# Holding the fourth chunk's query and key writes until the first head's maxima rows have landed, with unread matrix products in the prologue's last units

## Chip, core and metric

One core of one Trainium2 chip. The metric is the device time of one launch in microseconds (us). Times of single instructions are in us on the profile's own scale, which begins with the first instruction.

## What is computed

A transformer block on x of 2 x 1024 x 256 (B = 2, S = 1024, H = 256): modulation vectors from a small input c, a layer norm with scale and shift, causal attention with 16 heads of width 16, a gated residual, a second modulated layer norm, and a mixture of 16 experts (4 chosen for each token, plus a shared one) with a second gated residual.

```python
h = _layernorm(x) * (1 + ca) + sa
q, k, v = split(h @ W_qkv.T + b_qkv, 3)            # 16 heads of width 16
scores = where(causal, -inf, (q @ k.T) * scale)
x = x + ga * ((softmax(scores) @ v) @ W_out.T + b_out)
h = _layernorm(x) * (1 + cb) + sb
x = x + gb * moe(h)                                # routed experts + shared expert
```

## The kernel before

All 2048 tokens are on one core, cut into four chunks of 512 (NC = 4), chunks 0 and 1 for batch 0, chunks 2 and 3 for batch 1. The instructions are written by hand, one program for each engine, with semaphores between them; each engine runs its own program in order. SP (SyncE) has nothing but transfers and waits in its program: `dma_start` puts a transfer into SP's queue (q1 in the profile), and a `wait_ge` in front of it stops everything behind it in that program. ScalarE (ACT) has a queue of its own (q10), and uses it for three transfers only, below.

**Prologue** (from 0 to 89 us). For each chunk TensorE (PE) turns the normed tokens and makes the query and key projections, four tiles of 128 features x 512 tokens per chunk, each from 6 products of 512 columns (L2085, `hh` and `hl` are the high and low part of the activations, `Wqkh` and `Wqkl` of the weights). The results are split into three bf16 parts in the tile AP (`PT[c % 2]`), and SP writes each tile as three transfers of 384, 256 and 128 KB to the DRAM tensor qk_parts (`write_tile`, L795), so 12 transfers and 3 MB for a chunk. From there they are read back, head group by head group, as Qs and Ks (`stage`, L802 and L803). There are 8 head groups of four heads; groups 0 to 3 need chunks 0 and 1 alone.

**Attention** is one loop over the head groups n = 0 to 7, with two interleaved streams on PE in an order worked out beforehand: the `scores` of group n (L2166), whose exponentials ACT makes (L1377) and whose products with the values (`products`, L2152) follow, and the `score_unit`s of group n+1 (L2060 for the causal mask, L2062), 48 for each group, of which VectorE (DVE) only takes the row maxima (L1517). The maxima are turned by PE (`turn_max`, L2130), copied by DVE to the tile MT (L1633), and three small transfers of 4 KB (`aug`, L728) write them as three further rows under the queries in Qs, so that the scores come out with the maximum taken off. This is done for each half of the queries: `aug_in[slot][half]` counts the landings. A score of the first half waits for `aug_in[slot][0]`, and the first score of the second half (step s = 4 of 12) for `aug_in[slot][1]`.

For group 0 no attention runs beside the units: 36 of the 48 are interleaved with chunk 3's projections, and the last 12 (u = 36 to 47) stand alone, in the part `n == -1` of PE's body. In it the first half's maxima are turned after unit 40; ACT issues their three transfers on its own queue, while SP issues those of every other half.

SP's order around this place is: the 12 writes of chunk 2, the 12 of chunk 3, a wait until all of these have landed (L912), then Wg (L913) and three broadcast loads of the modulation rows (L916, 256 KB each), and then the first thing of attention, the maxima rows of group 0's second half (L728). After these come the loads for group 2.

A bank of PSUM, `pvb`, holds the sums of `products`; the first product of a group overwrites it. In the prologue it was used for the values, which were read by DVE before unit 41.

Of the kernel before, what the change touches and what calls it, by code (L numbers as in the profile page):

```python
# [15 lines left out]
P = 128  # L16
# [7 lines left out]
TPC = CH // P  # L24
HG = 4
# [67 lines left out]
UNITS = len(ROWS) * HG  # L93
# [60 lines left out]
OVER = PER * (4 * KH + 4)  # L154
# [19 lines left out]
}  # L174


IDLE_PE = {1: 16, 13: 10, 19: 4}


# [150 lines left out]
def program(nc, x, wqk, bqk, wv, bv, wout, bout, cT, wmod, wgate, wsh, wexp, qkd, modrows, hTd, xd, padd, zd, wd, out):  # L330
    with ExitStack() as ctx:

        def sem(name):
            return ctx.enter_context(nc.semaphore(name))
# [75 lines left out]
        hh = [early.put(f"hh{i}", [P, KH, CH], F32R) for i in range(2)]  # L410
        hl = [early.put(f"hl{i}", [P, KH, CH], F32R) for i in range(2)]
        Rq = [early.put(f"Rq{i}", [P, CH], F32) for i in range(2)]
        Wqkh, Wqkl = (early.put(n, [P, KH, 2 * H], F32R) for n in ("Wqkh", "Wqkl"))
# [108 lines left out]
        mbank, ebank, pvb, tb = allb[0:RING], allb[RING:2 * RING], allb[6], allb[7]  # L522
# [44 lines left out]
        aug_in = [[sem(f"aug_in{i}_{h}") for h in range(2)] for i in range(SLOTS)]  # L567
# [195 lines left out]
        def _(sp):  # L763
# [20 lines left out]
            def write_parts(c):  # L784
                for i in range(4):
                    write_tile(c, i)

            def write_tile(c, i):
                b, half, m = c // (S // CH), c % (S // CH), M_ORDER[i]
                sp.wait_ge(parts_done[b], 4 * half + i + 1)  # L790
                rows = qkd[m // KH, b, (m % KH) * P:(m % KH + 1) * P, :, half * CH:(half + 1) * CH]
                for first, count, part in PART_RUNS[m // KH]:
                    src = PT[c % 2][:, part:part + 1, m, :].broadcast_to([P, count, CH]) if m // KH else (
                        PT[c % 2][:, part:part + count, m, :])
                    sp.dma_start(rows[:, first:first + count, :], src).then_inc(parts_out[c % 2], 16)  # L795

            def stage(n, slot):

                q, k = (qkd[t].rearrange("b (g j d) i s -> (b g) (d i) j s", g=NG, j=HG)[n:n + 1].rearrange(
                    "a d j s -> (a d) j s") for t in range(2))  # L800
                for half in range(S // CH):
                    sp.dma_start(Qs[slot][0:NPR, half, :, :], q[:, :, half * CH:(half + 1) * CH]).then_inc(staged[slot], 16)  # L802
                sp.dma_start(Ks[slot][0:NPR, :, :], k).then_inc(staged[slot], 16)  # L803
# [85 lines left out]
            def body(n, at, first, last):  # L889
                if n == -1:  # L890

                    write_parts(0)
                    write_tile(1, 0)
                    write_tile(1, 1)
                    sp.wait_ge(parts_out[0], 16 * 12)
                    sp.wait_ge(parts_out[1], 16 * 6)
                    stage(0, 0)
                    write_tile(1, 2)
                    write_tile(1, 3)
                    stage(1, 1)  # L900
                    sp.wait_ge(v_read, 2 * (S // CH))
                    sp.wait_ge(const_done, N_CONST)
                    for s in range(SLOTS - 1):
                        stage_values(s, s)
                    sp.wait_ge(modrow_step, 7)
                    sp.dma_start(modrows, MR).then_inc(modrow_out, 16)

                    write_parts(2)
                    write_parts(3)
                    for i in range(2):  # L910
                        sp.wait_ge(parts_out[i], 16 * 12 * B)
                    sp.wait_ge(v_read, 2 * NC)  # L912
                    sp.dma_start(Wg[:, :, :], wgate).then_inc(wg_in, 16)  # L913
                    sp.wait_ge(modrow_out, 16)
                    for i, dst in enumerate((SBr, CBr, GBr)):
                        sp.dma_start(dst[:, :, :], modrows[:, i * H:(i + 1) * H].rearrange(  # L916
                            "(a b) h -> a b h", a=1).broadcast_to([P, B, H])).then_inc(modrow_in, 16)
                    return
                slot = at(0)[0]
                sp.wait_ge(bank_read["t"], USE[("max", n, 1)][1] + 1)  # L920
                aug(sp, slot, 1)
                for k in EARLY_LOADS.get(n, ()):
                    load_words(k)
                if n + SLOTS - 1 < NIT:

                    sp.wait_ge(e_ps, n * HEADS + 1)
                    sp.wait_ge(pv_done, n * NS + 1)
                    stage(n + (SLOTS - 1), (slot + SLOTS - 1) % SLOTS)
                    stage_values(n + (SLOTS - 1), (slot + SLOTS - 1) % SLOTS)
                for k in EARLY_RAW.get(n, ()):  # L930
                    load_raw(k)
                if not last:
                    sp.wait_ge(bank_read["t"], USE[("max", n + 1, 0)][1] + 1)
                    aug(sp, (slot + 1) % SLOTS, 0)
                if n == 0:
                    keep_pads()
                for k in EARLY_STORES.get(n, ()):
                    store_words(k)
                if n == 5:
                    for k in range(3):  # L940
                        load_words(k)
                if n in (5, 6):
                    store_turned(n - 5)
                if n == 7:
                    load_turned(0)
                    load_turned(1)
# [1073 lines left out]
        def _(pe):  # L2020
# [50 lines left out]
            for c in range(NC):  # L2071
# [7 lines left out]
                for i, m in enumerate(M_ORDER):  # L2079
                    n = 4 * c + i  # L2080
                    if n >= QK_RING:
                        pe.wait_ge(qk_read, 2 * (n - QK_RING + 1))
                    for k in range(KH):
                        for a, (w, h) in enumerate(((Wqkh, hh), (Wqkh, hl), (Wqkl, hh))):
                            ins = nc.tensor.matmul(allb[QK_RING + n % QK_RING], w[:, k, m * P:(m + 1) * P],  # L2085
                                                   h[c % 2][:, k, :], start=(k == 0 and a == 0),
                                                   stop=(k == KH - 1 and a == 2))
# [12 lines left out]
                for v in range(2):  # L2100
                    if c:
                        pe.wait_ge(v_read, 2 * (c - 1) + v + 1)
                    for u in range(2):
                        t0 = (2 * v + u) * P
                        for k in range(KH):
                            for a, (h, w) in enumerate(((hh, Wvh), (hl, Wvh), (hh, Wvl))):
                                ins = nc.tensor.matmul(allb[6 + v][:, u * H:(u + 1) * H], h[c % 2][:, k, t0:t0 + P],
                                                       w[:, k, :], start=(k == 0 and a == 0),
                                                       stop=(k == KH - 1 and a == 2))
# [15 lines left out]
            def turn_max_waits(n, half):  # L2125
                pe.wait_ge(mp_step, n * 9 + (9 if half else 4))
                before(pe, ("max", n, half))

            def turn_max():
                nc.tensor.transpose(tb.bitcast(BF16)[0:3 * HG * TPC, 0:P],  # L2130
                                    MP[:, :, :, :].rearrange("p a j i -> p (a j i)"), identb[:, :]).then_inc(mpT_ps, 1)
# [116 lines left out]
            def work(piece):  # L2248
# [15 lines left out]
                if what == "tab":  # L2264
                    spread_tables()

            def body(n, at, first, last):
                if n == -1:
                    for u in range(OVER, UNITS):
                        score_unit(0, 0, u)  # L2270
                        if u == max(OVER, HG * TPC) + HG:
                            pe.wait_ge(v_read, 2 * NC)
                            turn_max_waits(0, 0)
                            turn_max()
                    pe.wait_ge(qk_read, 2 * 4 * NC)
                    return
                (slot, turn), (nxt, nxt_turn) = at(0), at(1)
                pe.wait_ge(staged_v[slot], turn * 16 + 16)
                if not last:
                    pe.wait_ge(staged[nxt], nxt_turn * (16 * STAGE_DMAS) + 16 * STAGE_DMAS)  # L2280
                if last:
                    pe.wait_ge(m_red, NIT * UNITS)
                for what, i in ORDER:
                    if what == "scores":
                        scores(n, slot, turn, i)
                    if what == "unit" and not last:
                        score_unit(n + 1, nxt, i)
                    if what == "products":
                        if i == 0:
                            turn_max_waits(n, 1)  # L2290
                        if i == 5 and not last:
                            turn_max_waits(n + 1, 0)
                        if i >= 0:
                            products(n, slot, i)
                        elif n:
                            products(n - 1, at(-1)[0], NS - 1)
                    if what == "max" and (i == 1 or not last):
                        turn_max()
                    if what == "out" and (not last if i == 0 else n):
                        turn_out(2 * n - i)  # L2300
                    if what == "late":
                        if last and i == LAST_OUT:
                            turn_out(2 * n)
                        for piece in LATE_PE.get((n, i), ()):
                            work(piece)
# [66 lines left out]
            def idle_products(s):  # L2372
# [4 lines left out]
                else:  # L2377
                    was_read(pe, ("cnt",))
                    to = allb[0]
                for i in range(IDLE_PE[s]):  # L2380
                    nc.tensor.matmul(to[:, :], Wsh[:, 0:P], Wsh[:, P:P + CH], start=True, stop=True)

            for s in range(-1, SN):
                if s >= 0:
                    (s_multiply if S_ORDER[s][0] == "u" else s_down_tiles)(*S_ORDER[s][1:])
                if s in IDLE_PE:
                    idle_products(s)
# [140 lines left out]
```

## Time and profile before

| | |
|---|---|
| time of three runs | 651.31 us median (649.25 to 651.44) |
| span of the profiled execution, first to last instruction | 644.6 us |
| its own time | not given by the page; 6.7 us lie between its span and the median |
| busy in the span | PE 90%, DVE 76%, ACT 59%, POOL 52% |
| packets of SP's queue | 45.3% of the 16 DMA engines' time |
| last score unit of the prologue starts | 85.68 us |
| first score of attention starts | 89.32 us |
| first score of the second half starts | 99.47 us |

The shares are averages over the whole span. Around 60 to 87 us the DMA engines are full; at 86 to 89 us PE has nothing to run.

### The profile page before, as it was taken

How to read it: one execution, taken by the hardware profiler on the slowest of the kernel's cores; microseconds unless marked ns; L12 is line 12 of the kernel's file. 1: busy time of each engine (PE TensorE's matmuls, PEld its weight loads, DVE VectorE, ACT ScalarE, POOL GpSimd, SP SyncE). 2: the span in 40 equal slices, each digit the busy share in tenths (PEclk: the TensorE clock that was granted, in tenths of full speed). 3: DMA queues.
4: the chain of work that ended last, by engine and by line, in shares of the span. 5: the costliest groups of instructions: out<-in, count | busy, mean ns of one | idle time of the engine just before them, and what ended most of it. 6: DMA issues, size and time to landing. Idle time of an engine off the chain costs nothing. (4 is left out here: it accounts for less than half of the span.)

```text
span 644.6 us, 13664 instructions
## 1 busy us (share of the span) xinstructions
PE 582.1 (90%) x3960; PEld 395.7 (61%) x3960; DVE 487.5 (76%) x1415; ACT 382.8 (59%) x926; POOL 337.9 (52%) x585
## 2 busy tenths in 40 slices
PE   3879879999999999998997799997799999999996
PEld 3657533434343444444342378776799999999985
DVE  4888978888888868776967568898566766666648
ACT  3546437666766656655858552643356777776662
POOL 5524614455747527763738876774144444444430
PEclk9989969999999999998999989999799999999999
DMA  8349965961707273451305243665964444444498
GB/s 270 137 158 288 334 221 151 243 210 71 216 26 224 87 209 141 136 185 63 118 34 174 77 150 115 232 217 207 364 220 134 135 135 134 133 135 134 126 374 335
DMA packets 69066, 113.62 MB, mean 176 GB/s; under 512 B 12578, under 2 KB 51106, under 8 KB 67844
## 3 DMA queue, kind: packets, MB, share of 16 engines
q1 hardware_dynamic: 62036, 93.74, 45.3%
q0 software_dynamic: 6864, 19.01, 7.6%
q8 instruction: 34, 0.56, 0.4%
q14 instruction: 36, 0.29, 0.1%
q10 hardware_dynamic: 96, 0.01, 0.0%
HBM read 60.57 MB, written 49.94 MB: 171 GB/s over the span
## 5 line engine op out<-in xcount | busy, mean ns | idle before, releaser
L1377 ACT ACTIVATE Pr<-bank 128x512 f32<-128x512 f32 (+3 forms) x384 | 165.5, 494 | 94.8 <-PE bank L2166 91.1
L1517 DVE TENSOR_REDUCE mxA<-bank 128x1 f32<-128x128 f32 (+3 forms) x256 | 112.2, 484 | 23.9 <-PE bank L2062 23.7
L1233 POOL DMA_INDIRECT expert_rows<-Y,YIX x79 | 75.7, 959 | 104.0 <-DVE ytmp L1938 75.5
L2166 PE MATMUL bank<-Qs,Ks 99*128 99x512 bf16 (+3 forms) x384 | 118.6, 332 | 8.0 <-ACT Pr L1377 3.8
L2062 PE MATMUL bank<-Ks,Qs 96*128 96x512 bf16 (+3 forms) x384 | 122.1, 334 | 2.2 <-DVE mxA L1517 1.3
L1517 DVE TENSOR_REDUCE mxB<-bank 128x1 f32<-128x512 f32 x128 | 81.5, 681 | 13.5 <-PE bank L2062 13.4
L2152 PE MATMUL bank<-Pr,Vst 128*32 128x512 f32 (+3 forms) x768 | 83.4, 507 | 4.4 <-POOL Pr L1217 4.4
L1167 POOL DMA_INDIRECT chosen_rows<-Hx,pos x64 | 69.9, 1093 | 21.1 <-issue 17.5
L2415 PE MATMUL bank<-W,xh 128*128 x316 | 78.3, 329 | 0.4 <-issue 0.4
L1215 POOL TENSOR_TENSOR tick<-ident 128x1 f32<-128x1 f32 x128 | 25.4, 198 | 100.5 <-ACT Pr L1377 99.7
L2166 PEld LDWEIGHTS bank<-Qs,Ks 99*128 99x128 bf16 x384 | 36.0, 98 | 61.4 <-ACT Pr L1377 38.7
L2060 PE MATMUL bank<-mask,identb 128*128 128x128 bf16 x256 | 55.1, 227 | 7.7 <-DVE mxA L1517 5.3
L1968 DVE TENSOR_TENSOR act_a<-bank,sg 128x176 f32<-128x176 f32 x79 | 27.0, 342 | 45.3 <-ACT sg L1424 45.2
L2062 PEld LDWEIGHTS bank<-Ks,Qs 96*128 96x128 bf16 x384 | 38.1, 99 | 28.8 <-DVE mxA L1517 6.1
L1217 POOL TENSOR_SCALAR_AFFINE_SELECT Pr<-Pr 128x256 f32<-128x256 f32 x128 | 53.3, 416 | 0.0
L2415 PEld LDWEIGHTS bank<-W,xh 128*128 128x128 f32 x316 | 52.3, 189 | 1.3 <-issue 1.0
L2415 PE MATMUL bank<-W,xl 128*128 x158 | 51.3, 325 | 0.0
L1424 ACT ACTIVATE sg<-bank 128x176 f32<-128x176 f32 x79 | 25.1, 317 | 37.4 <-PE bank L2415 37.4
L2060 PEld LDWEIGHTS bank<-mask,identb 128*128 128x128 bf16 x256 | 25.1, 98 | 30.0 <-DVE mxA L1517 13.6
L1439 ACT ACTIVATE Y<-bank 128x256 f32<-128x256 f32 x79 | 30.3, 384 | 13.7 <-PE bank L2444 5.4
L1931 DVE TENSOR_TENSOR xl<-bank,xh 128x256 fp32r<-128x256 f32 x79 | 32.9, 416 | 5.8 <-ACT xh L1418 5.8
L2369 PE MATMUL bank<-ident,G 128*128 128x128 f32 x158 | 30.9, 278 | 6.0 <-DMA G<-chosen_rows 6.0
(254 smaller groups left out, 1314.8 us busy)
## 6 DMA issues: line engine op xcount, KB each, us to landing
G<-chosen_rows SPq DMA_DIRECT2D x79, 132.0 KB
Z<-expert_rows SPq DMA_DIRECT2D x16, 512.0 KB, 12.3
W<-expert_words SPq DMA_DIRECT2D x7, 1088.0 KB, 7.1
qk_parts<-AP SPq DMA_DIRECT2D x16, 384.0 KB, 5.0
Qs<-qk_parts SPq DMA_DIRECT2D x16, 384.0 KB, 4.2
Ks<-qk_parts SPq DMA_DIRECT2D x8, 768.0 KB, 9.0
Wraw<-in_wexp SPq DMA_DIRECT2D x9, 608.0 KB, 5.1
SA<-in_wexp SPq DMA_DIRECT2D x7, 608.0 KB, 10.5
```

The costliest lines, as they stand in the source:

```text
L1167: nc.gpsimd.indirect_dma_start(out=xd, out_offset=bass.IndirectOffsetOnAxis(ap=pos[:, c * TPC + t, j:j + 1], axis=0), in_=chosen(c)[:, t, ...
L1217: nc.gpsimd.affine_select(out=v, in_=v, compare_op=ALU.is_ge, fill=0.0, base=0, pattern=[[0, 2], [1, P]], channel_multiplier=-1).then_inc( ...
L1233: nc.gpsimd.indirect_dma_start(out=zd, out_offset=bass.IndirectOffsetOnAxis(ap=YIX[:, b:b + 1], axis=0), in_=Y[b % YRING], in_offset=None) ...
L1377: nc.scalar.activation(Pr[(2 * s + j // 2) % 4][:, j % 2, 0:w], ebank[p % RING][:, 0:w], ACT.Exp, scale=SCALE).then_inc(exp_done, EXP)
L1517: nc.vector.tensor_reduce(dst, mbank[u % RING][:, 0:w], AX.X, ALU.max).then_inc(m_red, 1)
L1931: nc.vector.tensor_tensor(xl[u % 2][:, :], xbank[:, 0:H], xh[u % 2][:, :].bitcast(F32), ALU.subtract).then_inc(xl_done, 1)
L2060: nc.tensor.matmul(mbank[u % RING][:, w - P:w], identb[:, :], mask[:, :], start=True, stop=False, skip_group_check=True)
L2062: nc.tensor.matmul(mbank[u % RING][:, 0:w], Qs[slot][0:NPR, i // TPC, j, (i % TPC) * P:(i % TPC + 1) * P], Ks[slot][0:NPR, j, k0:k0 + w], ...
L2152: ins = nc.tensor.matmul(pvb[32 * j:32 * j + 32, q0:CH], Vst[slot][:, kt, 32 * j:32 * j + 32], Pr[(2 * s + j // 2) % 4][:, j % 2, 0:w], st ...
L2166: nc.tensor.matmul(ebank[p % RING][:, 0:CH - q0], Ks[slot][0:NAUG, j, kt * P:(kt + 1) * P], Qs[slot][0:NAUG, qc, j, q0:CH], start=True, st ...
L2369: ins = nc.tensor.transpose(xbank[:, k * P:(k + 1) * P], G[u % GRING][:, k * P:(k + 1) * P], ident[:, :])
L2415: ins = nc.tensor.matmul(ubank[u % 2][:, 0:2 * EI], x_part[u % 2][:, k * P:(k + 1) * P], words(u, first + k * 2 * EI, 2 * EI), start=(k == ...
```

## The change

SP waits for the three landings of group 0's first maxima rows before it issues the twelve writes of chunk 3. PE gets products whose results nobody reads (high part of the weights by the high part of chunk 3's activations, 128 x 128 by 512 columns) after the units from 40 on: one after each of units 40 to 46, six after unit 47, so 13 in all. Their results go to `pvb`. Everything else stays.

```diff
+LAST_UNREAD = 6
 IDLE_PE = {1: 16, 13: 10, 19: 4}
...
                     write_parts(2)
+                    sp.wait_ge(aug_in[0][0], 16 * 3)
                     write_parts(3)
                     for i in range(2):
                         sp.wait_ge(parts_out[i], 16 * 12 * B)
...
+            def unread_products(n):
+
+                for i in range(n):
+                    nc.tensor.matmul(pvb, Wqkh[:, 0, 0:P], hh[1][:, 0, :], start=True, stop=True)
...
             def body(n, at, first, last):
                 if n == -1:
                     for u in range(OVER, UNITS):
...
                             pe.wait_ge(v_read, 2 * NC)
                             turn_max_waits(0, 0)
                             turn_max()
+                        if u >= max(OVER, HG * TPC) + HG:
+                            unread_products(1 if u < UNITS - 1 else LAST_UNREAD)
                     pe.wait_ge(qk_read, 2 * 4 * NC)
                     return
```

## Rows read from the trace of the kernel before

**Rows 1.** The page's first lines: the span, and PE's busy time.
```profile
span 644.6 us, 13664 instructions
PE 582.1 (90%) x3960; PEld 395.7 (61%) x3960; DVE 487.5 (76%) x1415; ACT 382.8 (59%) x926; POOL 337.9 (52%) x585
```

**Rows 2.** Waits from 88 to 100 us: who for whom, total, times, longest.
```profile
PE bank L2166 <- DMA Qs<-MT: 3.0, 1, 3.0
...
PEld bank L2166 <- DMA Qs<-MT: 0.4, 1, 0.4
```

**Rows 3.** Timeline from 80 us: start, length, engine, line, instruction, idle before it.
```profile
83.07 1.87 DVE L1517 TENSOR_REDUCE mxB<-bank 128x1 f32<-128x512 f32 x3
...
83.18 1.88 ACTq L728 DMA_DIRECT2D Qs<-MT  x3
...
85.68 0.63 PE L2062 MATMUL bank<-Ks,Qs 96*128 96x512 bf16 x1
...
89.32 0.59 PE L2166 MATMUL bank<-Qs,Ks 99*128 99x512 bf16 x1 [3.01 <-DMA Qs<-MT]
```

**Rows 4.** DMA queues from 83.2 to 86.4 us: packets, MB, share.
```profile
q1 hardware_dynamic: 1272, 1.23, 109.1%
```

**Rows 5.** DMA queues from 86.4 to 89.4 us.
```profile
q1 hardware_dynamic: 514, 0.48, 45.7%
q10 hardware_dynamic: 96, 0.01, 2.7%
```

**Rows 6.** Line 728 from 83 to 90 us, and from 96 to 100 us.
```profile
DMA to landing us min/median/max: 4.3/4.4/4.7
...
DMA to landing us min/median/max: 1.7/1.7/1.8
```

**Rows 7.** SP's timeline: first and last write of chunk 3, then what follows.
```profile
75.94 0.48 SPq L795 DMA_DIRECT2D qk_parts<-AP  x1
...
83.22 0.64 SPq L795 DMA_DIRECT2D qk_parts<-AP  x1
...
92.39 0.47 SPq L916 DMA_DIRECT2D GBr<-mod_rows  x1
96.28 1.89 SPq L728 DMA_DIRECT2D Qs<-MT  x3
```

**Rows 8.** SP's own wait for the writes of chunk 3.
```profile
SPq L912 <- DMA qk_parts<-AP: 5.5, 1, 5.5
```

**Rows 9.** Stretches: busy time of each engine, granted clock, DMA share, GB/s.
```profile
75.94:89.36 13.42, 7.69 (x31) 2.31 (x31) 12.17 (x31) 0.00 (x0) 0.00 (x0) 0.76 0.96 336
...
632.42:635.83 3.41, 2.17 (x11) 1.59 (x10) 3.27 (x6) 2.56 (x7) 0.00 (x0) 1.00 1.03 422
...
44.24:45.00 0.76, 0.76 (x3) 0.65 (x2) 0.72 (x2) 0.76 (x2) 0.13 (x1) 0.50 0.00 0
```

**Rows 10.** PE's timeline at the second half's first score.
```profile
99.47 0.39 PE L2166 MATMUL bank<-Qs,Ks 99*128 99x512 bf16 x1
99.69 0.38 PE L2062 MATMUL bank<-Ks,Qs 96*128 96x512 bf16 x1
```

**Rows 11.** PE's timeline at the lower clock, and ACT's exponentials of one step.
```profile
42.95 0.63 PE L2085 MATMUL bank<-hl,Wqkh 128*128 128x512 f32 x1
43.38 0.63 PE L2085 MATMUL bank<-hh,Wqkl 128*128 128x512 f32 x1
...
91.30 2.07 ACT L1377 ACTIVATE Pr<-bank 128x512 f32<-128x512 f32 x4
```

**Rows 12.** Stretches between changes of the granted clock (columns as in rows 9).
```profile
79.46:82.88 3.42, 1.84 (x8) 0.50 (x6) 3.32 (x11) 0.00 (x0) 0.00 (x0) 1.00 1.09 384
...
86.29:89.70 3.41, 0.40 (x2) 0.13 (x2) 1.92 (x7) 0.00 (x0) 0.00 (x0) 0.50 0.47 160
89.70:93.11 3.41, 3.41 (x20) 2.30 (x19) 1.93 (x7) 3.09 (x5) 0.56 (x2) 0.50 0.18 36
93.11:96.53 3.42, 3.42 (x27) 1.68 (x26) 2.77 (x8) 2.15 (x6) 1.64 (x6) 1.00 0.69 206
```

## The prediction

> **What bounds the kernel now.** I read the page first. PE is busy for 90% of the span [rows 1], so in attention and the experts a delay on PE moves the end by as much, and a microsecond in which PE stands still is worth a microsecond. I then looked for the place of the change in the list of waits. PE waits once, for 3.0 us, before the first score of attention, for the transfers Qs<-MT [rows 2]. The timeline shows the two sides of it: DVE has written MT and ACT issues the three transfers from 83.18 to 85.06, the last of them at about 84.4; PE starts its last unit at 85.68, is free at about 86.3 and starts scoring at 89.32 [rows 3]. Then the queues: from 83.2 to 86.4 all packets are q1's, SP's writes, and the engines are full; all 96 packets of q10, ACT's queue, run from 86.4 on, though they were issued before [rows 4, 5]. From issue to landing they take 4.3 to 4.7 us, where the same three transfers take 1.7 us at 96 us, with nothing beside them [rows 6]. So the first scores wait because the maxima rows stand behind chunk 3's writes. The change goes after that.
>
> What I looked at next is SP's own program, since the new wait stops everything behind it. Before, SP issues chunk 3's writes from 75.94 to 83.86, waits 5.5 us until they have landed, at 89.36, issues Wg and the three modulation loads up to 92.86, then waits for MT, and issues the maxima rows of group 0's second half at 96.28 [rows 7, 8]. PE wants these at the first score of the second half: it waits only 0.4 us for them and starts it at 99.47 [rows 2, 10]. So SP has 3.4 us to spare there (92.86 to 96.28), and PE none.
>
> **The release.** Without chunk 3's writes in the engines the maxima rows take 1.7 us instead of 4.4 to 4.7: the last, issued at about 84.5, lands at 86.2, and SP goes on at 86.3. Chunk 3's first write moves from 75.94 to 86.3, by 10.4 us.
>
> **The writes.** They are 3 MB (12 transfers, 3.15 million bytes). The engines move 384 GB/s when they have nothing but such writes (79.46 to 82.88) [rows 12], so 8.2 us. From empty engines the bytes begin about 0.8 to 1.0 us after the first issue (44.24 to 45.00) [rows 9]. And the end is thin: from 86.4 to 89.4 only 0.48 MB went where 384 GB/s would have moved 1.15, which is 1.7 us lost [rows 5]. With all three the landing is 10.9 us after the first issue. The other way: before it took 13.42 us, in which 336 GB/s moved 4.51 MB, so 1.36 MB of earlier work stood ahead, worth 3.5 us; 9.9 us remain [rows 9], without the start that was hidden behind that work. I take the middle, 10.4: all writes have landed at 96.7. Issuing isn't the limit: 12 issues of some 0.5 us are 6 us. The bounds are 8.5 us (the highest rate of the trace, 422 GB/s, 7.5 us, with 1.0 to start and no thin end) and 10.9.
>
> **What is queued behind.** SP then needs what it needed before from 89.36 to 92.86, 3.5 us for Wg and the modulation loads [rows 7], and is ready for the second half's maxima rows at 100.2. MT is ready before that: it was 7.0 us after the first score before (89.32 to 96.28), and that score moves forward if anything. From the first of the three issues to PE's score it took 3.19 us (96.28 to 99.47) [rows 7, 10], so that score comes at 103.4 instead of 99.47: 3.9 us later. Bounds: 94.8 (landing) + 3.5 + 3.2 = 101.5, less 0.4 if the release comes that much sooner, so 1.6 us later at least; and at most 97.2 + 3.5 + 3.2 with the MT transfers held up 2.7 us by the modulation loads in front of them (4.4 instead of 1.7 us, as rows 6 show for full engines), so 7.1 us later. I take 3.9, near the lower end, because a single 256 KB load is much less than the backlog of rows 4.
>
> **PE's own shift is swallowed.** PE may start attention earlier: after its last unit, 86.3, or, with six unread products of 0.22 us behind a unit at the full clock, at 87.2. It comes to the second half 9.75 us after its first score (99.47 less 89.32 less the 0.4 waited), at 97.0, and stands until 103.4. What it gains of the 3.0 us is lost there. SP's writes can't be passed: PE runs in order, and nothing of group 0's second half can go ahead.
>
> **The unread products.** Each is 0.22 us at the full clock and 0.43 us at the lower one by the distance between the starts of products of 512 columns [rows 10, 11]. At the lower clock a unit (512 columns, with a mask of 128: 0.53 us) and a product take 0.96 us, where DVE needs 0.62 for a unit's reduction (1.87 for three) [rows 3]; the seven between the units then add up to 2.5 us and the six at the end 2.6, and attention starts at about 90 at the latest. Even then PE is at the second half's first score at 99.7, before 103.4. I cost the products at nothing: the wait for the maxima rows hides them, and without it they would cost 0.9 us (87.2 for 86.3) at the full clock. They may keep the clock from falling: it is 1.00 (2.4 GHz) up to 82.88 with PE busy 1.84 of the last 3.42 us, and 0.50 (1.2 GHz) until 93.11 [rows 12]. That too ends ahead of the new wait.
>
> **The clock behind the new wait.** PE would stand still from 97.0 to 103.4, 6.4 us, longer than the 3 us of before. In rows 12 the clock is at 0.50 through such a stretch and the busy one after it, and is back at 93.11, 3.8 us after PE's restart at 89.32. I expect the same again at 103.4. There a head's step needs two products of 512 columns on PE, 0.44 us at the full clock and 0.86 at the lower, and 0.52 us on ACT (2.07 for four) [rows 10, 11]. The lower clock makes each step 0.86 instead of 0.52, so 40% of 3.8 us is lost: 1.5 us. Bounds: 0, if it restarts at the full clock, and 3 us for twice the stretch.
>
> **Sum.** 3.9 + 1.5 = 5.4 us later from the second half of group 0 on. PE is busy nearly throughout behind it, and SP's later loads wait for PE's own progress, so I see nothing that gives it back. The profiled span is 644.6 us, so 650.0; the median stands 6.7 us above the span, and 651.3 + 5.4 = 656.7 us.
>
> **Rivals.** *The writes are hidden after all, and it is faster.* PE starts at 87.2 instead of 89.32, 2.1 us sooner, and saves perhaps 0.5 us more by the full clock in the first steps, a third of the 1.5 us above, since ACT's first exponential comes only at 91.30, 2 us after the first score: 648.7 us. For it speaks the wait of 3.0 us, which is real. It decides if SP has the second half's rows out at 94.2, so if the writes have landed at 90.7, 4.4 us after the release. For 3.15 MB that would be over 900 GB/s once the start of 1 us is off; the highest stretch shows 422 [rows 9]. It needs a much earlier release. I give it 0.09.
>
> *A small loss.* The writes run near the upper rate and the restart costs no clock: 1.6 to 3.2 us, 653.7 us. The rates of rows 9 differ by 10%, and the clock's behaviour depends on where the pause falls. 0.18.
>
> *The maxima rows don't come sooner.* If their 4.4 us are not due to SP's writes, they land at 89.3 as before, SP starts the writes 3.0 us later than I have it, and the same chain gives 3.9 + 3.0 + 1.5 = 8.4 us, 659.7 us. Against it stand rows 4 to 6: no packet of q10 before 86.4. The Trainium skill speaks for it: "DMA: Bandwidth & Descriptors", section "Queues, rings and completion order", says that each DMA engine takes turns between the queues that have work, a packet at a time, so three small transfers of ACT's queue should hardly wait for SP's. By that rule holding the writes back would bring nothing; rows 4 and 5 show the opposite order here. Together with a longer stretch at the lower clock after the pause I give this side 0.13.
>
> My own case has 0.60, with 654.6 to 658.8 us as its range.
>
> **Numbers.** About 0.5%, 3.3 us, is what a measurement of this kernel tells from no change. Slower by more: 0.60 + 0.13 = 0.73. Within: the small loss, 0.18. Faster: 0.09. The range reaches down to 652.9, the lower bound of 1.6 us without the clock's loss, and up to 660.3, the late release with a little more, and leaves out the faster case and the end of the late one, 0.15 together.
>
> **What the profile would show.** Right: packets of q10 within 2 us of their issue at 83 to 85; chunk 3's writes issued from about 86.3; the wait of L912 ending at 96 to 97; L728 from SP at about 100; the first score of attention at 87 to 88; and a wait of 5 to 7 us of L2166 for Qs<-MT at the second half, with the granted clock at 0.50 after it. Wrong: if L912 ends before 92, or if PE's wait at the second half is under 2 us. And if the end moves by less than the second half's first score does, something behind it had slack that I don't see.

## The result and the profile after

The changed kernel takes 656.24 us (median of 5 runs, 654.89 to 656.92), the kernel before 650.81 us on the same chip (5 runs, 649.25 to 651.44): 5.4 us more, ratio 1.0067 with a 95% interval of 1.0041 to 1.0093, so 2.7 to 6.1 us. The forecast was 656.7 us. Ratios and intervals, here and below, leave out slow runs (one of the kernel before, 768.57 us, and six in the last series), so a ratio need not be the quotient of the medians beside it.

PE's timeline of the changed kernel: start, length, line, instruction, and the idle time before it. Lines up to 908 have a number one higher than before, those from there to 2266 one that is two higher (L795 is L796 now, L2166 is L2168).

```profile
88.75 0.39 PE L2168 MATMUL bank<-Qs,Ks 99*128 99x512 bf16 x1
...
97.66 0.64 PE L2154 MATMUL bank<-Pr,Vst 128*32 128x256 f32 x8
103.96 0.61 PE L2168 MATMUL bank<-Qs,Ks 99*128 99x512 bf16 x1 [5.65 <-DMA Qs<-MT]
```

The first scores do start earlier, at 88.75 instead of 89.32, and with no wait. But at the first score of the second half PE now stands still for 5.65 us, where it waited 0.4 us before, and comes 4.49 us later than in [rows 10]. SP's timeline and its own waits show why:

```profile
87.75 0.36 SPq L796 DMA_DIRECT2D qk_parts<-AP  x1
...
98.16 0.35 SPq L915 DMA_DIRECT2D Wg<-in_wgate  x1
98.57 0.42 SPq L918 DMA_DIRECT2D SBr<-mod_rows  x1
...
99.54 0.47 SPq L918 DMA_DIRECT2D GBr<-mod_rows  x1
100.06 1.89 SPq L729 DMA_DIRECT2D Qs<-MT  x3
...
115.39 1.15 SPq L729 DMA_DIRECT2D Qs<-MT  x2
```
```profile
SPq L796 <- DMA Qs<-MT: 11.8, 1, 11.8
SPq L914 <- DMA qk_parts<-AP: 2.9, 1, 2.9
```

Against [rows 7]: chunk 3's first write goes from 75.94 to 87.75, the landing of all of them from 89.36 to 98.1, and the second half's maxima rows from 96.28 to 100.06. In [rows 8] SP's wait at that place was for the writes; now it stands 11.8 us for the first half's rows before it issues anything, and 2.9 us for the writes behind them.

The granted clock over the same part, stretch by stretch (busy time of PE, PEld, DVE, ACT, POOL; then the granted clock, the share of the DMA engines, GB/s):

```profile
79.00:82.33 3.33, 1.61 (x9) 0.57 (x7) 3.23 (x11) 0.00 (x0) 0.00 (x0) 1.00 0.18 62
82.33:85.74 3.41, 3.41 (x10) 1.55 (x10) 2.97 (x6) 0.00 (x0) 0.00 (x0) 0.50 0.04 7
85.74:88.75 3.01, 3.01 (x16) 1.77 (x16) 2.73 (x6) 0.00 (x0) 0.00 (x0) 1.00 0.04 12
...
98.30:103.90 5.60, 0.00 (x1) 0.00 (x0) 0.81 (x4) 0.00 (x0) 5.07 (x10) 0.90 0.53 163
103.96:109.63 5.67, 5.67 (x25) 2.25 (x26) 3.27 (x6) 3.55 (x7) 0.65 (x3) 0.50 1.05 274
109.63:115.39 5.76, 5.76 (x41) 2.00 (x39) 4.51 (x11) 3.74 (x7) 0.00 (x0) 1.00 0.24 79
```

In [rows 12] the clock was at 0.50 from 82.88 to 93.11. It is now at 0.50 for 3.41 us only, since the unread products fill PE's gaps, and is back before the first score. The price comes behind the new pause: 5.67 us at 0.50, from 103.96 on. From the second half's first score to the next maxima rows (SP's L728, now L729) it takes 11.43 us (103.96 to 115.39); in the kernel before the same work took 9.51, all at the full clock:

```profile
99.47:108.98 9.51, 9.41 (x67) 3.48 (x64) 8.24 (x21) 6.70 (x13) 5.82 (x14) 1.00 0.79 222
```

So at that point the kernel is 6.4 us late (115.39 less 108.98), 4.5 from the pause and 1.9 from the clock behind it. The last of attention's maxima rows are still 5.8 us late (347.70 after, 341.87 before). The spans of the two profiled executions, 655.2 and 644.6 us, differ by 10.6 us, so by another 4.8 us in what follows. That part does not seem to be the change's: behind the last maxima rows the profile of before has 302.7 us, that of after 307.5, and two experiments below, whose times are those of the kernel before, have 306.1 (E3: 646.7 less 340.55) and 306.5 (E2: 650.9 less 344.41). The profiled execution of before was an unusually short one at its end.

### The profile page after: what moved, and what is told of

It is laid out like the page before. It is cut to its first block and busy times, and to the rows that moved or that the text cites. A ratio compares the mean times of both kernels' runs of the same rounds, so it can differ in the third digit from the quotient of the medians.

```text
span 655.2 us, 13691 instructions
## 1 busy us (share of the span) xinstructions
PE 590.6 (90%) x3973; PEld 401.8 (61%) x3973; DVE 489.4 (75%) x1415; ACT 383.8 (59%) x926; POOL 339.6 (52%) x585
## 5 line engine op out<-in xcount | busy, mean ns | idle before, releaser
L2168 PE MATMUL bank<-Qs,Ks 99*128 99x512 bf16 (+3 forms) x384 | 118.8, 333 | 10.8 <-DMA Qs<-MT 5.7
L2168 PEld LDWEIGHTS bank<-Qs,Ks 99*128 99x128 bf16 x384 | 36.1, 98 | 64.7 <-ACT Pr L1379 39.6
L1219 POOL TENSOR_SCALAR_AFFINE_SELECT Pr<-Pr 128x256 f32<-128x256 f32 x128 | 54.7, 427 | 0.0
```

Of the source, the lines that this page charges most:

```text
L1219: nc.gpsimd.affine_select(out=v, in_=v, compare_op=ALU.is_ge, fill=0.0, base=0, pattern=[[0, 2], [1, P]], channel_multiplier=-1).then_inc( ...
L2168: nc.tensor.matmul(ebank[p % RING][:, 0:CH - q0], Ks[slot][0:NAUG, j, kt * P:(kt + 1) * P], Qs[slot][0:NAUG, qc, j, q0:CH], start=True, st ...
```

## Experiments

The ratios are to the kernel before, run beside each experiment in one of three series, in which it took 650.88 us (E1 to E4), 650.37 us (E5 to E8) and 663.73 us (E9 to E11 and the full change again). Single runs of one kernel scatter over 4 to 11 us in a series, and the intervals reach 1 to 3 us to either side, so a difference of 1 or 2 us between two experiments is not told apart by their times; only the traces show such differences, and each trace is of one execution.

**E1: the wait alone.** The thirteen unread products are taken out.

```diff
-                        if u >= max(OVER, HG * TPC) + HG:
-                            unread_products(1 if u < UNITS - 1 else LAST_UNREAD)
```

> The new wait on SP alone, without the thirteen unread products. My theory (the loss is SP's: chunk 3's writes and what follows them push the second half's maxima rows back, and the products are hidden behind PE's pause) says that the first score of the second half still starts at 103 to 104 us, and that the time is that of the full change, 656 us, within 1 us, some 5 us above before. The rival, that the products cost something of their own, says 1 us or more below the full change.

Measured: 656.63 us against 650.88, ratio 1.0089 (1.0054 to 1.0125). As slow as the full change. PE's timeline, and the stretch around the first scores:

```profile
86.33 0.59 PE L2168 MATMUL bank<-Qs,Ks 99*128 99x512 bf16 x1
...
104.03 0.61 PE L2168 MATMUL bank<-Qs,Ks 99*128 99x512 bf16 x1 [4.96 <-DMA Qs<-MT]
```
```profile
80.82:94.47 13.65, 12.30 (x49) 4.98 (x53) 11.73 (x31) 5.53 (x9) 1.65 (x6) 0.50 0.58 201
```

The whole loss is the wait's. The products add nothing to the time here, and the lines show what they do: without them attention starts at 86.33, 2.4 us sooner than with them, but at the lower clock until 94.47, and it comes to the second half at 99.07 (104.03 less 4.96), 0.8 us later than with them (98.3). Either way PE then stands until 104.

That both stand until 104 has a part that I had not seen. Without the products the first half's rows landed 1.7 to 1.8 us after their issue and SP issued chunk 3's first write at 86.21, 1.5 us sooner than in the full change. But the landing of all of them was at 98.1 in both: without the products the engines moved only 25 GB/s from 95.5 to 98.1, a sixteenth of the 384 GB/s before, as if one engine of 16 had been left behind (an estimate from the rate). So two differences of 1.5 us cancel. Why that end is thin for so long is not shown.

**E2: the products alone.** SP's new wait is taken out.

```diff
-                    sp.wait_ge(aug_in[0][0], 16 * 3)
```

> The thirteen unread products alone, with SP's order as before. My theory: the maxima rows land at 89.3 as before and cover the products, the second half's first score stays at 99.5, and the time is that of before (650.8) within 1 us. The rival, that the products delay PE or DVE beyond that cover (at the lower clock up to 0.7 us by the sum, more if the clock stays low), says 652 us or more; a gain of 1 us or more would say that holding the clock up is worth something by itself.

Measured: 650.74 us against 650.88, ratio 0.9979 (0.9952 to 1.0006). No difference that can be told; the interval reaches from a gain of 0.5% to a loss of 0.1%. The time came as expected, the trace did not: in the profiled execution (653.65 us, the slowest of the twelve) PE waits 1.44 us for the first half's rows, starts at 90.18 and comes to the second half at 101.09, where I had expected 99.5. The next maxima rows are issued at 110.60, 1.6 us later than before. The median shows nothing of that, and whether the faster executions had this delay isn't known.

**E3: the second half's maxima rows directly behind chunk 3's writes**, before SP waits for their landing and loads the modulation rows.

```diff
                     sp.wait_ge(aug_in[0][0], 16 * 3)
                     write_parts(3)
+                    sp.wait_ge(bank_read["t"], USE[("max", 0, 1)][1] + 1)
+                    aug(sp, 0, 1)
                     for i in range(2):
                         sp.wait_ge(parts_out[i], 16 * 12 * B)
...
-                sp.wait_ge(bank_read["t"], USE[("max", n, 1)][1] + 1)
-                aug(sp, slot, 1)
+                if n:
+                    sp.wait_ge(bank_read["t"], USE[("max", n, 1)][1] + 1)
+                    aug(sp, slot, 1)
```

> The full change, but SP issues the second half's maxima rows directly behind chunk 3's writes, before it waits for their landing and loads the modulation rows. My theory: the rows are issued at about 95.2 to 97.1 and land at 98.5 to 99.5, PE's pause there falls from 5.65 us to about 1 us, the clock stays up behind it, and the time is 650 to 651.5 us, 5 to 6 us below the full change. The rival, that it is the traffic of the writes and not the order behind them that holds the second half up, says that most of the 5.65 us stay and the time is above 654 us.

Measured: 650.32 us against 650.88, ratio 0.9988 (0.9969 to 1.0007). PE at the second half, and SP's issue:

```profile
98.79 0.39 PE L2171 MATMUL bank<-Qs,Ks 99*128 99x512 bf16 x1 [0.49 <-DMA Qs<-MT]
```
```profile
87.80 7.42 SPq L796 DMA_DIRECT2D qk_parts<-AP  x12
95.67 1.92 SPq L729 DMA_DIRECT2D Qs<-MT  x3
```

E3 settles the cause. The writes are as late as in the full change and as large, but what stood behind them in SP's program no longer waits for them, and the loss is gone. It is the order behind the wait, not the traffic, that costs 5.4 us. It also shows what the change brings in this form: the second half starts at 98.79, 0.7 us ahead of [rows 10], and that is not to be seen in the time.

**E7: the rows ahead of the loads, but behind the landing.** To part the two things that stood in front of the rows.

```diff
                     for i in range(2):
                         sp.wait_ge(parts_out[i], 16 * 12 * B)
+                    sp.wait_ge(bank_read["t"], USE[("max", 0, 1)][1] + 1)
+                    aug(sp, 0, 1)
                     sp.wait_ge(v_read, 2 * NC)
                     sp.dma_start(Wg[:, :, :], wgate).then_inc(wg_in, 16)
```

(and as in E3 only `if n` in the loop)

> The full change, with the second half's maxima rows issued behind the landing of chunk 3's writes as in it, but ahead of Wg and the three modulation loads. It separates the two terms in front of the rows. In the profile of the full change these loads take SP from 98.16 to 100.0 and their bytes stand ahead of the rows: my theory says that the rows start at 98.2, PE's pause is 3 us instead of 5.65, and the time is 653 to 654 us, so half of the loss is the loads and half the landing. The rival, that the landing alone sets it, says 655.5 or more.

Measured: 654.12 us against 650.37, ratio 1.0041 (1.0020 to 1.0061), so 3.8 us above before, where the full change is 5.4.

```profile
101.47 0.39 PE L2171 MATMUL bank<-Qs,Ks 99*128 99x512 bf16 x1 [3.19 <-DMA Qs<-MT]
```

The pause falls from 5.65 to 3.19 us and the second half starts 2.5 us sooner than in the full change; with the landing out of the way too it starts another 2.7 us sooner (98.79 in E3). So in the trace the four loads and the landing have about half each, as expected. In the time the two halves can't be told apart: the intervals of E7 and of the full change overlap.

**E5 and E10: the clock kept up through the pause.** 24 and then 18 unread products ahead of the second half's first score.

```diff
                     if what == "scores":
+                        if n == 0 and i == HG * TPC:
+                            was_read(pe, ("max", 0, 1))
+                            for _ in range(PAUSE_UNREAD):
+                                nc.tensor.matmul(tb, Ks[0][0:NPR, 0, 0:P], Ks[0][0:NPR, 0, 0:CH], start=True, stop=True)
                         scores(n, slot, turn, i)
```

> The full change, and in PE's pause ahead of the second half's first score 24 further unread products of 512 columns (to the bank of the turned maxima, which has been read by then), 5.2 us at the full clock in a pause of 5.65 us. They change nothing but PE's activity in the pause. My theory puts 1.5 to 2 us of the loss on the lower clock behind the pause: the granted clock stays at 1.00 there, the second half's first score stays at 104.0, and the time is 654.3, 1.5 to 2 us below the full change. The rival, that the lower clock is hidden behind ScalarE there, says no difference to the full change (656.2).

Measured with 24: 656.70 us against 650.37, ratio 1.0088 (1.0056 to 1.0120), so nothing won that can be told, with runs from 650.7 to 659.4. In its profile the products ran past the rows' landing, and the second half started at 104.95. The clock stayed at 1.00, and the next maxima rows were issued at 114.22, 1.2 us sooner than in the full change. I repeated it with fewer, and the full change beside it:

> The full change once more, unaltered, beside the next three on the same chip: 656 us, 5 us above before, with PE's pause of 5 to 6 us ahead of the second half's first score. It is the measure for the run with 18 products in the pause, since the one with 24 gave 656.7 us where 654.3 was expected, with a spread of 9 us.

> The full change with 18 unread products in PE's pause (3.9 us of it at the full clock) instead of 24, which ran 1 us over the end of the pause. My theory: first score of the second half at 104, granted clock 1.00 behind it, the maxima rows of group 1 issued 1.9 us earlier than in the full change (113.5 instead of 115.4), and a time 1.5 to 2 us below the full change of the same call. The rival, that the clock's share is lost again further on or is nothing, says a time within 0.5 us of it.

In this series the kernel before took 663.73 us, some 13 us longer, so only its own numbers are compared. In the profiles the additional time lies behind attention: the last maxima rows are issued at 348.73 in the full change, where it was 347.70, and its span is 671.1 us instead of 655.2. The full change again: 667.36, ratio 1.0050 (1.0016 to 1.0084). With 18 products in the pause: 666.73, ratio 1.0036 (1.0001 to 1.0070). The stretch from the second half's first score to the next maxima rows, and a later one, first of the run with 18 products, then of the full change:

```profile
103.76:113.04 9.28, 9.19 (x63) 3.48 (x64) 7.48 (x17) 6.68 (x13) 0.85 (x4) 1.00 0.82 223
341.81:355.46 13.65, 13.14 (x57) 3.50 (x56) 7.92 (x36) 9.30 (x24) 9.98 (x24) 0.50 0.39 126
```
```profile
104.36:116.04 11.68, 11.68 (x63) 4.42 (x64) 7.90 (x17) 7.29 (x13) 0.87 (x4) 0.73 0.61 174
341.81:355.46 13.65, 10.98 (x90) 3.71 (x87) 8.46 (x37) 11.20 (x30) 10.91 (x26) 1.00 0.36 106
```

At its place the clock's share is shown: 9.28 us instead of 11.68 for the same work, 2.4 us. In the time it isn't decided: the medians differ by 0.6 us, but each ratio is only known to some 0.35%, 2.3 us to either side, so neither the 1.5 to 2 us that I expected nor nothing is excluded. In this profile nearly the whole gain is lost again in attention (last maxima rows at 348.39 and 348.73), and a visible part of it at 341.81, where the clock is at 0.50 for 13.65 us in which it was at 1.00 in the other. E7, which has no products in the pause, shows the same stretch (0.50 for 13.65 us from 341.40), so it isn't special to them. Whether it follows from a shift or is chance, these runs don't tell.

**E11: SP's wait ended when the rows are made, not when they have landed.**

```diff
-                    sp.wait_ge(aug_in[0][0], 16 * 3)
+                    sp.wait_ge(bank_read["t"], USE[("max", 0, 0)][1] + 1)
```

> The full change, with SP's wait ended when the maxima rows have been made (MT copied, 83.1) instead of when they have landed (87.7). Chunk 3's writes start 4.4 us sooner, beside ScalarE's three small transfers. My theory: the writes have landed by 93.7, the modulation loads are issued by 95.6, the second half's rows at 96, and PE has a pause of at most 1.5 us: 650 to 652 us, 4 to 6 us below the full change. The small transfers land at 87.5 to 88.5, since little stands in front of them. A rival: the writes overtake them as in the kernel before, they land at 89 or later, and the gain at the start is gone, but not the rest: 651.5 to 653 us.

Measured: 663.53 us against 663.73, ratio 0.9979 (0.9943 to 1.0015), 3.8 us below the full change of this series. The writes start at 83.88, 3.9 us sooner than in the full change, and PE's pause is shorter:

```profile
83.88 7.90 SPq L796 DMA_DIRECT2D qk_parts<-AP  x12
95.28 0.35 SPq L915 DMA_DIRECT2D Wg<-in_wgate  x1
```
```profile
101.73 0.61 PE L2168 MATMUL bank<-Qs,Ks 99*128 99x512 bf16 x1 [2.63 <-DMA Qs<-MT]
```

So a shorter wait of SP takes the loss away, which the intervals show (1.0016 to 1.0084 with the full wait). How much of it per microsecond they don't show: in the trace the second half starts 2.6 us sooner than in the full change of this series (104.36), still 2.3 us later than in [rows 10], and the next maxima rows are issued 4.2 us later than before (113.21), though the times are the same. The profiled execution was one of its slowest, 666.26 us. The pause was to be 1.5 us at most and is 2.63. The small transfers landed 2.7, 2.7 and 4.2 us after their issue, against 4.3 to 4.7 behind the full queue of [rows 6] and 1.7 to 1.8 in E1. The slowest was there at about 89.4 and attention started at 89.56, so of the gain at the start nothing was left, as the rival said.

**E4: chunk 3's writes behind the second half's rows as well.** SP issues these first, with no wait for the first half's rows.

```diff
                     write_parts(2)
-                    sp.wait_ge(aug_in[0][0], 16 * 3)
+                    sp.wait_ge(bank_read["t"], USE[("max", 0, 1)][1] + 1)
+                    aug(sp, 0, 1)
                     write_parts(3)
```

(and as in E3 only `if n` in the loop)

> Chunk 3's writes wait for the second half's maxima rows as well: SP issues those first and the writes behind them, the unread products stay. My theory: the first scores start at 88 to 89 us, the second half's at 97.5 to 98.5 with no pause, 1 to 2 us before its place in the kernel before, and the time is 649 to 650 us. Against it stands what then is late: the loads of group 2 start 12 us later and would land at about 118 us, with PE asking for them at about 119; if they miss it, PE pauses there and the time is that of before or more.

Measured: 660.67 us against 650.88, ratio 1.0161 (1.0131 to 1.0190). The expected gain was there, with the second half at 98.41, and then it was lost, at PE's next two waits for maxima rows:

```profile
123.34 0.38 PE L2170 MATMUL bank<-Qs,Ks 99*128 99x512 bf16 x1 [3.33 <-DMA Qs<-MT]
139.10 0.61 PE L2170 MATMUL bank<-Qs,Ks 99*128 99x512 bf16 x1 [4.70 <-DMA Qs<-MT]
```
```profile
122.75 5.89 SPq L833 DMA_DIRECT2D chosen_rows<-PADZ  x1
128.68 2.60 SPq L834 DMA_DIRECT2D chosen_rows<-PADM  x1
131.33 6.57 SPq L729 DMA_DIRECT2D Qs<-MT  x3
```

What I had named against it, group 2's loads, is one step short: they and the modulation loads stand ahead of group 1's first rows, which take 9.3 to 9.7 us from issue to landing instead of 1.7, and push the 4 MB of padding rows (L829 to L834) to where group 1's second rows are due. The three transfers of 4 KB then take SP 6.57 us to issue instead of 1.8.

**E6 and E8: the rows ahead of the last tile's three writes**, with and without the unread products.

```diff
-                    write_parts(3)
+                    for i in range(3):
+                        write_tile(3, i)
+                    sp.wait_ge(bank_read["t"], USE[("max", 0, 1)][1] + 1)
+                    aug(sp, 0, 1)
+                    write_tile(3, 3)
```

(and as in E3 only `if n` in the loop)

> The full change, but SP issues the second half's maxima rows behind nine of chunk 3's twelve writes, and the last tile's three behind them. The rows are issued as soon as the maxima are there (94.7) and have at most 1 us of writes ahead in the engines. My theory: they land at 97 to 97.5, PE comes to the second half at 98 with no pause, 1.5 us ahead of the kernel before, and the time is 649.3, 1.5 us below before and 1 us below the version with all twelve in front. A rival: the last tile lands later, SP's loads of group 2 with it, and something there gives the gain back, so 650.3 or more.

> The version with the rows ahead of the last tile, without the thirteen unread products. With no pause behind to swallow them the products now count. My theory: PE starts the first scores at 86.3 instead of 88.7 but at the lower clock up to 93 or 94.5, and comes to the second half 0.5 to 1 us later than with the products (the run with the wait alone came there 0.7 us later than the full change): 0 to 1 us above the version with products. The rival, that the products delay the start more than the clock gives back, says 0.5 us or more below it.

Measured: 653.68 us, ratio 1.0061 (1.0037 to 1.0084), and 653.76 us, ratio 1.0054 (1.0033 to 1.0076), against 650.37. My expectation of a gain in E6 was wrong and its rival right. PE reached the second half at 99.28, not at 98, and then the same thing happened as in E4, smaller: Wg, the modulation loads and those of group 2 come 3.9 us later than in E3, the padding rows behind them take longer and meet the next maxima rows, and PE waits.

```profile
127.21 5.43 SPq L729 DMA_DIRECT2D Qs<-MT  x3
```
```profile
133.85 0.39 PE L2173 MATMUL bank<-Qs,Ks 99*128 99x512 bf16 x1 [2.79 <-DMA Qs<-MT]
```

The products make no difference between the two that can be told (0.1 us; 0 to 1 was expected, which these intervals don't test).

**E9: E6 with the padding rows moved to group 1.**

```diff
-                if n == 0:
-                    keep_pads()
...
+                if n == 1:
+                    keep_pads()
                 for k in EARLY_RAW.get(n, ()):
                     load_raw(k)
```

> The version with the rows ahead of the last tile (653.7 us), with the 4 MB of padding rows that SP writes in group 0 moved to group 1, behind its second maxima rows and the loads of group 3. In that version these rows took 5.4 us to issue at 127.2 behind the padding writes, and PE waited 2.8 us. My theory: that wait goes, and with it 2.8 us and the clock behind it, so 649 to 650.5 us. The rival: the padding writes meet the next rows in group 1 in the same way, and the time stays at 652 us or more.

Measured: 682.88 us against 663.73, ratio 1.0283 (1.0237 to 1.0328). PE's wait for the rows issued at 127 is gone, as expected, and a much longer one takes its place. The waits from 127 to 182 us:

```profile
POOL SH L1184 <- DMA SA<-in_wexp: 23.7, 1, 23.7
...
PE bank L2159 <- POOL Pr L1224: 18.4, 1, 18.4
```

The first expert words, which GpSimd splits in its own order between the causal masks, are loaded behind the padding rows; GpSimd waits 23.7 us for them, and PE 18.4 us for the mask behind that. The rival I had written down named the wrong victim.

## Why the prediction was right

**The release.** Right in kind: the first half's rows no longer stand behind the writes, their packets run from 84.6 on instead of 86.4. The size was off by 1.4 us. I took 1.7 us from issue to landing from [rows 6], and the slowest took 3.1, so SP went on at 87.75 instead of 86.3. In E1 and E8, which have no unread products, the three took 1.7 to 1.8 us and SP went on 3.0 us after the first issue (at 86.21 in E1), which is my figure; in the full change it was 4.4 us. So the products, costed at nothing, seem to cost the 1.4 us of the release; what the traces show of the reason stands at the end.

**The writes.** From the first issue to the landing 10.4 us were taken, and it is 10.35 (87.75 to 98.1). The middle of two workings met it, but not each term: the bytes begin 0.9 us after the first issue, run 8.2 us, and the thin end is 1.2 us (97 to 98.1), not 1.7. E1 took 11.9 us (86.21 to 98.1), which is outside my bounds of 8.5 to 10.9. That the end of this sum came out is luck: with the release at 86.3, as I had it, E1 still landed at 98.1 and not at 96.7.

**What is queued behind.** Right, and E3 shows it: with the rows taken out from behind, the loss is gone. Its parts were off against each other. Wg and the modulation loads took 1.9 us, not the 3.5 of [rows 7], where the issue of the load for SBr took 1.58 us (0.42 now); from the rows' issue to the score it was 3.9 us, not 3.19, since the loads' bytes stood in front of them (E7, with the rows ahead of the loads, has 3.09). The landing was 1.4 us late, the loads gave 1.6 us back, and the last step took 0.7 us more. The score was to come at 103.4 and came at 103.96: 4.5 us instead of 3.9.

**PE's own shift is swallowed.** Right: PE was to be there at 97.0 and was at 98.3, and stood until the rows came. E1, which starts attention 2.4 us sooner than the full change, has the same time.

**The products.** Costed at nothing, and E1 and E2 show no cost in the time. The reason given was only the wait that hides them; their effect on the release was not seen. The bound for the lower clock was also added up wrongly: 86.3, 2.5 and 2.6 us give 91.4 for the start of attention, not about 90, and 101.1 for the second half, not 99.7, which is still ahead of 103.4. That they bring the clock back by 85.74 instead of 93.11 was held possible; it is worth 0.8 us of arrival beyond their own length (E1), and no effect on the end can be told.

**The clock behind the wait.** 1.5 us were taken for 3.8 us at the lower clock; it was 5.67 us and cost 1.9 us at the next maxima rows, 2.4 in the second pair (E10). Whether this reaches the end of the kernel is open. E5 and E10 took the lower clock away, and their times can't be told from that of the full change, but 2 us can't be told in them either.

**The sum.** 5.4 us forecast and 5.4 measured. The agreement is better than the terms are, and in part luck: the release, the loads and the last step were off by 1.4, 1.6 and 0.7 us and nearly cancel, the place in attention is 6.4 us late, 5.8 at its end, and the measured difference itself is known to 2.7 to 6.1 us. What the experiments bear out is the mechanism, the second half's rows held behind SP's wait. Of the signs named beforehand, the wait of 5 to 7 us, the clock at 0.50 after it, the rows at about 100 and the packets within 2 us came as said; the first writes (87.75), their landing (98.1) and the start of attention (88.75) each came later than said.

**The rivals.** The faster case needed the landing by 90.7; it was 98.1. The small loss needed a restart at the full clock; it was at 0.50. The late case needed maxima rows that come no sooner; SP went on at 87.75, ahead of 89.3. The rule of the Trainium skill, "DMA: Bandwidth & Descriptors", section "Queues, rings and completion order", that an engine takes turns between its queues, was to mean that three small transfers hardly wait for SP's queue. The traces don't agree with that: the holding back helps (first packets at 84.6 instead of 86.4), and from issue to landing the rows took 4.3 to 4.7 us beside the full queue and 1.7 to 1.8 us with it empty (E1). Even beside writes that were issued together with them they took 2.7 to 4.2 us (E11).

## What to carry to other kernels

A wait put into a queue that runs in order has to be costed by the first urgent thing behind it, not by the transfers that it holds back: here it was three transfers of 4 KB, due 10 us later. Where such a wait is wanted, move the urgent small transfers ahead of everything that waits for the large ones (E3), and follow the queue further than the next consumer: E4, E6 and E9 each cured one wait and made another 15 to 40 us later. Work that only keeps the clock up brought no gain here that could be told, and it seems to have delayed small transfers beside it.

## What the runs showed that I had not expected

- Three small transfers on ScalarE's queue, with SP's queue empty, took 1.7, 2.2 and 3.1 us to land (minimum, median, maximum) in the changed kernel, and 1.7 to 1.8 in E1 and E8, which leave out the unread products. Three transfers of the same size from SP's queue took 1.7 to 1.8 in [rows 6].

```profile
DMA to landing us min/median/max: 1.7/2.2/3.1
```

The queues from 83 to 86 us in the changed kernel show one thing that E1 doesn't have there, a transfer of instructions:

```profile
q8 instruction: 1, 0.02, 2.9%
q10 hardware_dynamic: 90, 0.01, 2.3%
```

Its 2.9% of 16 engines' 3 us would be 1.4 us on one engine (an estimate). In this window 90 of the 96 packets of q10 run; the last six come from 86 us on, where E1 has all 96 done by then. In E1 this transfer of instructions comes behind the rows' landing, at about 88. So my reading is that the thirteen products bring the next load of instructions forward, into the rows' way. It fits all ten runs that hold the writes back until the rows have landed: in the eight with the products the slowest row took 3.1 to 3.5 us, in E1 and E8 without them 1.8. No run tests it by itself.

- SP's issue of small transfers can take much longer than elsewhere (1.8 to 2.0 us for three): 6.57 us in E4 and 5.43 in E6, both directly behind the padding rows' 4 MB. Full engines alone don't do it: in E4 the three at 112.50 took 1.86 us to issue, though they then took over 9 us to land.
- A gain of 2.4 us in one place of PE's own stream, seen in the trace, was down to 0.3 us at the end of attention in the same two profiles (E10). One profile of each can't say whether that is the rule.
